# Attention of a macaron block: DVE's additions, row moments and routing steps put ahead of the first maxima of a step

## The reference

```
x = x + 0.5 * ffn(layernorm(x))      # 64 experts, top 8 of them from 4 of 8 groups, and a shared one
x = x + attention(layernorm(x))      # 16 heads of 64, causal, softmax over 256
x = x + 0.5 * ffn(layernorm(x))
```

## Time and profile before

| | us |
|---|---|
| median of 3 runs (1705.00 to 1706.74) | 1705.74 |
| the profiled execution, its own time | 1704.02 |
| its span from first to last instruction | 1702.3 |
| attention, from about 566 to 1183 of the span | about 617 |

### The profile page before, as it was taken

One profiled execution on the slowest core, in us unless ns is written; L12 is line 12 of the kernel. 1 busy time (PEld: TensorE's weight loads), 2 busy tenths in 40 slices (PEclk: granted clock), 3 DMA queues, 4 the chain that ended last, 5 costly groups with the idle time before them and its releaser, 6 DMA issues. The chain is left out here.

```text
span 1702.3 us, 27254 instructions
## 1 busy us (share of the span) xinstructions
PE 1583.8 (93%) x8683; PEld 1021.4 (60%) x8683; DVE 1195.8 (70%) x3446; ACT 777.5 (46%) x2105; POOL 672.1 (39%) x931
## 2 busy tenths in 40 slices
PE   5899999998999899888889898999898999999999
PEld 2444444445888677666667666776347887444443
DVE  4687888663555577878787788765695855778665
ACT  2333223222444577666666666676223543223222
POOL 1000188885000334333333303371883001888840
PEclk9899999998999899999999999999999999999999
DMA  9998555552666101000000000011555664666652
GB/s 185 190 257 219 151 129 129 144 142 78 168 186 186 52 21 28 23 22 18 21 20 19 18 1 20 26 52 34 142 144 139 184 189 136 148 144 154 146 133 62
DMA packets 202043, 181.31 MB, mean 107 GB/s; under 512 B 39408, under 2 KB 154288, under 8 KB 201904
## 3 DMA queue, kind: packets, MB, share of 16 engines
q1 hardware_dynamic: 175056, 132.34, 32.7%
q0 software_dynamic: 16384, 33.59, 7.3%
q10 hardware_dynamic: 10464, 13.63, 2.4%
HBM read 121.83 MB, written 57.67 MB: 105 GB/s over the span
## 5 line engine op out<-in xcount | busy, mean ns | idle before, releaser
L840 ACT ACTIVATE f_hid<-banks 128x512 f32<-128x512 f32 (+1 forms) x264 | 157.6, 597 | 506.9 <-PE banks L800 506.7
L481 POOL DMA_INDIRECT x_rows<-r_xk,r_idx x256 | 266.2, 1040 | 125.8 <-issue 53.6
L862 DVE TENSOR_TENSOR f_hid<-banks,f_hid 128x512 f32<-128x512 f32 (+1 forms) x264 | 181.5, 688 | 150.1 <-ACT f_hid L840 149.8
L812 PE MATMUL banks<-f_hid,wd 128*128 128x512 f32 x528 | 272.8, 600 | 10.1 <-DVE f_hid L875 10.1
L796 PE MATMUL banks<-r_xT_d,gu 128*128 128x512 f32 x528 | 276.4, 606 | 4.8 <-DMA wd<-in_L_ffn_We_down 3.2
L800 PE MATMUL banks<-r_xT_d,gu 128*128 128x512 f32 x528 | 272.8, 598 | 0.0
L875 DVE TENSOR_TENSOR f_hid<-f_mix_wide,f_hid 128x512 f32<-128x512 f32 x256 | 175.7, 686 | 30.7 <-DMA f_mix_wide<-mix_rows 28.4
L517 POOL DMA_INDIRECT a_g<-y_rows,r_idx x128 | 127.2, 994 | 172.2 <-POOLq L1602 106.0
L517 POOL DMA_INDIRECT f_g<-y_rows,r_idx x128 | 129.1, 1008 | 162.6 <-DMA y_rows<-f2q_yq 133.0
L812 PEld LDWEIGHTS banks<-f_hid,wd 128*128 128x128 f32 x528 | 99.7, 192 | 143.7 <-issue 122.1
L800 PEld LDWEIGHTS banks<-r_xT_d,gu 128*128 128x128 f32 x528 | 101.0, 191 | 130.2 <-issue 126.4
(11 more groups left out here) (237 smaller groups left out, 2839.4 us busy)
## 6 DMA issues: line engine op xcount, KB each, us to landing
f_mix_wide<-mix_rows SPq DMA_DIRECT2D x124, 512.0 KB, 6.9
x_rows<-zero ACTq DMA_DIRECT2D x12, 1024.0 KB, 6.5
f1q_xq<-x_rows SPq DMA_DIRECT2D x48, 256.0 KB, 3.1
y_rows<-f1q_yq SPq DMA_DIRECT2D x48, 256.0 KB, 2.4
f2q_xq<-x_rows SPq DMA_DIRECT2D x48, 256.0 KB, 3.1
y_rows<-f2q_yq SPq DMA_DIRECT2D x48, 256.0 KB, 2.4
x_rows<-r_xk,r_idx POOLq DMA_INDIRECT x256
wd<-in_L_ffn_We_down SPq DMA_DIRECT2D x7, 512.0 KB, 10.7
```

The source lines that it names most:

```text
L481: nc.gpsimd.indirect_dma_start(x_rows[:, :], bass.IndirectOffsetOnAxis(ap=b.idx[:, f, CT * k + t, j:j + 1], axis=0), b.xk[:, k, t, :], Non ...
L812: mm = nc.tensor.matmul(acc[:, :], w["wd"][0:rows, 2 * p, :], d.hid[0:rows, g % HIDS, :], start=(p == 0), stop=(p == PAIRS))
L840: nc.scalar.activation(d.hid[0:rows, g % HIDS, :], gate_bank[g % 3][0:rows, :], ACT.Silu)\
L862: nc.vector.tensor_tensor(d.hid[0:rows, g % HIDS, :], up_bank[g % 3][0:rows, :], d.hid[0:rows, g % HIDS, :], ALU.mult).then_inc(gated, 1)
```

## The change

Inside DVE's `slot`, the additions, both kinds of moments and `routing(k)`, in this order, now stand ahead of the first maxima. Between the two maxima only `update_x` is left. The sigmoid is taken one step later, at FRONTS+10, where before it stood at FRONTS+9. No instruction is added or removed, and the other engines' programs are unchanged.

```diff
             def routing(k):
 
-                if front_row(k, 9) is not None:
-                    front_sigmoid(front_row(k, 9))
+                if front_row(k, 10) is not None:
+                    front_sigmoid(front_row(k, 10))
...
                 if k % QUADS == 1 and b_now + 1 < NB:
                     ln_apply(b_now + 1)
+                for i in lists_of(k - ADD_LAG):
+                    add(i // TOPK, (i % TOPK,), chunk_of)
+                if moments_row(k) is not None:
+                    ln_moments(moments_row(k))
+                if front_row(k, 6) is not None:
+                    front_moments(front_row(k, 6))
+                routing(k)
                 if live:
                     maxima(c, k, 0)
                 if k % QUADS == 1 and k >= LEAD_A:
                     update_x(c, k)
-                routing(k)
-                for i in lists_of(k - ADD_LAG):
-                    add(i // TOPK, (i % TOPK,), chunk_of)
                 if live:
                     maxima(c, k, 1)
                 if k % QUADS == 1 and b_now + 1 < NB:
                     xT_low(b_now + 1, (k // QUADS + 1) % 2)
-                if moments_row(k) is not None:
-                    ln_moments(moments_row(k))
-                if front_row(k, 6) is not None:
-                    front_moments(front_row(k, 6))
```

## The result

The changed kernel takes 1680.4 us (median of 4, 1676.98 to 1682.43) against 1705.37 for the kernel before in the same measurement: ratio 0.985, interval 0.983 to 0.987, 25 us less. The forecast was 1687.5, with a range from 1678 to 1704.

What follows compares the result with a forecast made beforehand. Bound: path from first maxima through extra work, second maxima, moments, `copy_o` and PE back to first maxima. Attention -20.7, clock +2.5, so -18.2 from 1704.0: 1685.8; that execution lies 1.7 below the median, so 1687.5, range 1678 to 1704.

Steps and rivals of the forecast that it cites:

- The path: Attention steps with DVE late: 1.22 + 4.77 us through exponentials to the last normalisation, plus X: 5.99 + X.
- the forecast's own work ahead of the maxima: X, DVE work between last normalisation and next first maxima: 4.57, 2.64, 3.25, 2.69, 4.96, 2.19, 1.54, 1.54 us, steps 14 to 21.
- Rival (b): Way from first maxima over exponentials to last normalisation exceeds 5.99: at 6.6 no gain, 1705; at 7.0, 1725; slower 0.14.
- One sign: In the profile after, PE's wait moves from `copy_o` to the scores or transposes; it was 46.5 us.
- The light steps: Attention steps with little DVE work: DVE may be 1.47 us late without holding up PE's 8.35, so they pay back heavy ones.
- The special steps: Steps 17 and 21: ACT first waits for `update_x`, a conversion and the logits' exponential, 1.34 us more; 12.29 and 12.39.
- 299.3: Steps 14 to 45, four groups of eight: 299.3 us against 319.2 before, a gain of 19.9.
- The ranks: Steps 48 to 51: placing waits for PE's ranks, holding up the first maxima; 10.94 us a step, 12.1 at 49.
- 20.7: Attention's total gain before the clock: 19.9 us from steps 14 to 45, 0.3 from 9 to 13, 46 to 51 62.9 against 63.4.

Runs made afterwards that it cites:

- The padding: Three extra scratch DVE instructions ahead of the first maxima, steps 14 to 45: ratio to the kernel before 0.994 in the changed kernel, 1.001 in the kernel before.
- the kernel with the moments behind: The changed kernel with both kinds of moments moved back behind the second maxima: ratio 0.980 to the kernel before.

## Why the prediction was right

The path. Forecast: a step in which DVE is late takes 5.99 us plus the work ahead of the next first maxima. Step 14 took 8.53 (8.63 forecast), 15 took 9.31 (9.24), 16 took 8.47 (8.68), 18 took 8.09 (8.18), 19 took 7.39 (7.53). Less the forecast's own work ahead of the maxima, these give 5.78 to 6.06 in place of 5.99. The padding shows a slope of about one in the changed kernel and of nothing in the kernel before. Rival (b), a longer way back to the normalisation, needed 6.6 and is refuted. One sign came only in part: PE's wait did not leave `copy_o` (19.1 us), and only 10.0 us stand at the transposes.

The light steps. That they pay back a heavy one held: step 19 took less than PE's own 8.35, step 20 took 8.60 (8.05 forecast, perhaps since step 19 had already left no lateness), and the steps from 52 on are what they were.

The special steps. The 1.34 us beyond an ordinary step (its bounds 0 and 1.97) was too much: ACT's exponentials started 2.01 us behind the first maxima, so it was 0.79. Step 17 took 11.50, not 12.29. The 0.55 too much, at steps 17, 25, 33 and 41, makes 2.2 of the 5.0 us by which steps 14 to 45 came out shorter than forecast (294.3 against 299.3). The rest of these 5.0, the most of it in the last group of eight (72.1 against some 74.3), was not traced. The ranks below took 1.1 us more than forecast the other way, so the 3.4 us between the forecast 20.7 and the 24.1 that attention gained are a difference of errors.

The ranks. Forecast 10.94 us at 47, 48 and 50, 12.1 at 49; measured 11.04, 11.66, 11.03 and 11.58; 46 to 51 took 64.0, not 62.9. DVE's wait is 6.9 us in all four, and undoing the placing and the count together gave 5.6, of which steps 43 and 44 are 1.5. The forecast had said that this part loses.

What the forecast did not ask is which part of the change earns the gain. The additions alone bring as much as the whole change (32 us on the chips of the experiments), but not because the rest is worth nothing: the routing ahead of the first maxima brings some 17 more there, in part by the clock, and the moments and the placing with the count give back 9 and 6. The later sigmoid has a share only if nothing else moves. The moments lay between the second maxima and `copy_o`, where DVE in the changed kernel waits for exponentials anyway. The wait for ranks was hidden behind the first maxima's own place in the order.

## What to carry to other kernels

An engine that idles in front of one instruction and is late behind it has room for as much work as its idle time there, and work added or moved there up to that much is nearly free; beyond it every added microsecond costs about its full length. Work that is moved beyond it can still pay, as the routing did, since it is gone from the place that it left: weigh both places. Sort the moved pieces by what they wait for: work whose input another engine makes late in the same step must not stand ahead of what that engine's next step needs. To find out whether there is room, put a known piece of scratch work into the place and see if the step grows. And try the parts of a change one by one: here a total of 25 us hid two parts that cost.

## What the runs showed of the hardware that was not expected

The same kernel took 1705 us in the first measurement and 1845 to 1849 on the three chips of the experiments. In a stalled step of the latter (step 8 of the kernel with the moments behind), DVE's maxima and what POOL did meanwhile:

```profile
653.69 0.42 DVE L1476 TENSOR_REDUCE a_top<-banks 128x2 f32<-128x256 f32 x1 [0.40 <-PE banks L1204]
...
656.56 0.95 POOL L517 DMA_INDIRECT a_g<-y_rows,r_idx  x1 [0.30 <-issue]
...
657.82 0.96 POOL L517 DMA_INDIRECT a_g<-y_rows,r_idx  x1 [0.31 <-issue]
...
660.15 0.42 DVE L1476 TENSOR_REDUCE a_top<-banks 128x2 f32<-128x256 f32 x1 [5.17 <-remote]
```

POOL issues one indirect DMA every 1.3 us throughout, while DVE stands 5.17 us in front of the second maxima with "remote", no instruction of this core, as the releaser. What it waits for stays open, and so does whether the chip makes the difference or something else that changed after the first measurement. The ratio of the changed kernel to the one before was 0.985 in both.

Three instructions of the same form and shape took 0.65 us in the padding and 0.95 as additions; a single one took 284 ns against 352 (medians). The two differ in several things: the padding reads one tile twice, multiplies by a constant and writes to places of its own, while each addition reads gathered rows, a weight for each row and x, and waits for the addition before it. Which of these makes the difference was not tried.
